# Reordered loads, scatter pacing and joined halves in a four-stage mixture-of-experts kernel

## What is computed

```
x = x + tanh(g0) * E(layernorm(x), token_ids, ctx)      # 4 experts, one per token, weights Wg = Wu = Wd = ctx[e], 512x512
x = x + tanh(g1) * F(layernorm(x))                      # gated FFN, 512 -> 2048 -> 512, Walsh-Hadamard transforms around its weights
x = x + tanh(g2) * R(layernorm(x), ctx)                 # a recurrence along the 512 positions of each sequence, per channel
x = x + tanh(g3) * M(layernorm(x))                      # 8 experts of 512 -> 448 -> 512, top 2 per token, and a shared expert
```

## Time and profile before

| what | value |
|---|---|
| runs | 1247.7, 1248.07, 1249.19 us, median 1248.07 |
| the profiled execution | 1258.69 us, of it the span 1256.9 us |
| PE busy | 1204.7 us, 96% of the span |
| DVE, ACT, POOL busy | 673.6, 453.4, 459.3 us |
| mean DMA rate | 194 GB/s |

### The profile page before, as it was taken

The page is one execution under the profiler, slowest core; times in us unless marked ns, Lnnn a source line. Parts: engine busy times, 40 slices in busy tenths (PEclk is TensorE's granted clock), DMA queues, the critical chain, the costliest instruction groups (busy, mean ns, idle before and its releaser), DMA issues.

```text
span 1256.9 us, 17870 instructions
## 1 busy us (share of the span) xinstructions
PE 1204.7 (96%) x5791; PEld 1012.7 (81%) x5792; DVE 673.6 (54%) x1231; ACT 453.4 (36%) x767; POOL 459.3 (37%) x397
## 2 busy tenths in 40 slices
PE   6799989999999999999999988998899999999998
PEld 6688868888888878888788877887688888888887
DVE  5655479766355665656455646868526333333331
ACT  3433343443234424343244327652122222222222
POOL 2232023000022210321233414353667537986665
PEclk9899999999999999999999999999899999999999
DMA  7842168755659955894786503125454525645553
GB/s 244 305 143 76 43 209 319 275 202 212 256 210 311 339 203 201 293 353 164 253 301 243 181 0 114 47 83 198 190 187 159 168 86 193 209 138 180 179 157 129
DMA packets 64955, 243.61 MB, mean 194 GB/s; under 512 B 8444, under 2 KB 10712, under 8 KB 51192
## 3 DMA queue, kind: packets, MB, share of 16 engines
q1 hardware_dynamic: 41144, 155.93, 33.9%
q0 software_dynamic: 23280, 86.55, 21.2%
q10 hardware_dynamic: 464, 0.27, 0.1%
HBM read 165.13 MB, written 77.59 MB: 193 GB/s over the span
## 4 chain that ended last, share of the span: by engine, by line
PE 82%; DVE 7%; issue 4%; ACT 3%; DMA 3%; POOL 1%; SPq 0%; ACTq 0%; DVEq 0%; POOLq 0%
PE bank L1281 25%; PE bank L1451 18%; PE bank L1307 12%; PE bank L1484 9%; PE bank L1219 4%; PE bank L1240 4%; PE bank L1414 2%; PE bank L1469 2%; PE bank L1262 1%; DMA xres<-in_ctx 1%; DMA wdn<-in_L_ffn_W_down 1%; POOL xs_sorted L824 1%; PE bank L1227 1%; PE bank L1197 1%; PE bank L1316 1%
## 5 line engine op out<-in xcount | busy, mean ns | idle before, releaser
L1281 PE MATMUL bank<-xTh,G 128*128 128x512 f32 x1024 | 272.6, 394 | 0.0
L1281 PEld LDWEIGHTS bank<-xTh,G 128*128 128x128 f32 x1024 | 190.8, 188 | 41.0 <-issue 2.4
L1451 PE MATMUL bank<-W,dxh 128*128 (+2 forms) x880 | 204.6, 373 | 13.5 <-DVE dmid L1942 7.9
L1451 PEld LDWEIGHTS bank<-W,dxh 128*128 128x128 f32 x880 | 161.8, 189 | 29.3 <-issue 15.8
L1307 PE MATMUL bank<-DN,bhh 128*128 128x512 f32 x512 | 158.0, 390 | 0.0
L1281 PE MATMUL bank<-xTl,G 128*128 128x512 f32 x512 | 137.1, 389 | 0.0
L1484 PE MATMUL bank<-W,dhh 128*128 (+1 forms) x440 | 126.9, 411 | 2.3 <-ACT dys L1103 2.1
L1795 DVE SCALAR_TENSOR_TENSOR bs<-bank,tab,bs 128x512 f32<-128x512 f32 x64 | 46.8, 732 | 146.8 <-PE bank L1281 146.8
L1940 DVE TENSOR_TENSOR dmid<-bank,dsg 128x384 f32<-128x384 f32 x55 | 30.5, 555 | 158.3 <-ACT dsg L1093 145.3
L1307 PEld LDWEIGHTS bank<-DN,bhh 128*128 128x128 f32 x512 | 96.1, 188 | 20.8 <-issue 1.0
L1281 PEld LDWEIGHTS bank<-xTl,G 128*128 128x128 f32 x512 | 96.1, 188 | 20.4
(11 more groups left out here) (296 smaller groups left out, 1963.0 us busy)
## 6 DMA issues: line engine op xcount, KB each, us to landing
G<-gate_up_split SPq DMA_DIRECT2D x48, 1024.0 KB, 7.1
DN<-down_split SPq DMA_DIRECT2D x24, 1024.0 KB, 4.9
gate_up_split<-G SPq DMA_DIRECT2D x16, 1024.0 KB, 6.3
wst<-in_L_ffn_w POOLq DMA_DIRECT2D x16, 896.0 KB, 5.6
y_all<-dys SPq DMA_DIRECT2D x55, 256.0 KB, 2.0
xs_sorted<-zero POOLq DMA_DIRECT2D x3, 3328.0 KB, 20.2
xsd<-xs_sorted SPq DMA_DIRECT2D x39, 256.0 KB
down_split<-DN SPq DMA_DIRECT2D x8, 1024.0 KB, 4.3
```

The costliest lines, as they stand in the source:

```text
L1281: mm = pe.matmul(bank[m][:, :], G[:, c % 2, f, h, m, i, :], a[b % 2][:, i, :], start=(n == 0), stop=(n == 3 * DC - 1))
L1451: mm = pe.matmul(bank[o][:, 0:width], a[par][:, k, :], w[:, bass.ds(slot, 1), at + k * step:at + k * step + width].rearrange("p a n -> p ( ...
```

## The change

In stage 1 SP loads all four matrices of ctx before W_down, and only three pieces of W_down before the first tile; PE and ACT run 6 calls of `w16` before the first tile, 6 after the last and 4 after the turns, instead of 10, 4 and 2. DVE runs more of `w_low` before the first tile. POOL computes the first `rstd` before a gather instead of after it, and reads a count earlier. In batches 1 to 3 the input of `mix` is cut into halves on ACT and DVE and multiplied in two `fp32r` matmuls, and the steps of `normal`, `turn` and the second `half_mix` move. In stage 3 the blocks of rows are spread otherwise over the tiles, and `d_hid` of tile 10 moves ahead of `places`. Between stages 3 and 4 the first routed tile waits for part of the scatters only, and PE's order around it changes.

```diff
-        BESIDE = 10
+        BESIDE = 6
...
-            sp.dma_start(nat_at[0], ctx_v[:, 0, :, :]).then_inc(s_ctx[0], 16)
+            for e in range(E0):
+                sp.dma_start(nat_at[e], ctx_v[:, e, :, :]).then_inc(s_ctx[e], 16)
             for n in range(BESIDE // 2):
                 sp.dma_start(wdn_at[n], w_down[:, 8 * n:8 * n + 8, :]).then_inc(s_wdn[n], 16)
-            sp.dma_start(nat_at[1], ctx_v[:, 1, :, :]).then_inc(s_ctx[1], 16)
...
-            sp.wait_ge(s_xg[0], 16)
-            for e in range(2, E0):
-                sp.dma_start(nat_at[e], ctx_v[:, e, :, :]).then_inc(s_ctx[e], 16)
             sp.wait_ge(s_wl, E0 * DC)
-            sp.wait_ge(s_w16, 8)
+            sp.wait_ge(s_w16, BESIDE)
             sp.wait_ge(s_rank, 2)
-            for n in range(BESIDE // 2, 8):
+            for n in range(BESIDE // 2, 7):
...
+                if t == NT0 - 2:                                   # SP, stores of stage 1
+                    sp.wait_ge(s_xn, NT0)
+                    sp.dma_start(wdn_at[7], w_down[:, 56:64, :]).then_inc(s_wdn[1], 16)
...
-            for t in range(TT - 2):                                # SP, stage 3
+            for t in range(TT - 3):
                 store(t)
+            sp.wait_ge(s_slot1, 2)
+            n = sp.value_load(first_i[0:1, 0:1], min_val=1, max_val=4)
+            for i in range(8):
+                sp.wait_ge(s_rsc[i], n * 16)
+            load(TT)
             for i in range(8):
                 sp.wait_ge(s_rsc[i], 16 * 2 * TT // 8)
-            load(TT)
             load(TT + 1)
+            store(TT - 3)
...
-            for j in range(DC):                                    # ACT, stage 1
+            for j in range(E0 * DC):
                 w_high(j)
...
-            for n in range(4):
+            for n in range(BESIDE):
                 w16(n)
-            for n in range(4, 8):
-                w16(n)
-                w_high(n)
             x_high(0)
-            for n in range(8, BESIDE):
-                w16(n)
             x_high(1)
-            for j in range(2 * DC, E0 * DC):
-                w_high(j)
...
+            def mix_high(b, h):                                    # ACT
+                act.wait_ge(s_bq, 2 * b + 2)
+                act.activation(xTh[b % 2][:, 2 * h:2 * h + 2, :], xq[b % 2][:, 2 * h:2 * h + 2, :], ACT.Copy).then_inc(s_xmh, 1)
...
+                if b < NB - 1 and k == (NK - 2 if b == 0 else 11): # ACT, after silu(g)
+                    mix_high(b + 1, 0)
+                    mix_high(b + 1, 1)
...
-            for n in range(2):                                     # PE, before the product of line 1189
-                w16(n)
...
-            for n in range(2, 8):
+            for n in range(BESIDE):
                 w16(n)
             x_turn(0)
-            for n in range(8, BESIDE):
-                w16(n)
             x_turn(1)
...
+                    pe.wait_ge(s_xml, 2 * b - 1 + c // 2)          # PE, mix for b > 0
+                    pe.matmul(bank[bk][:, :], signs[:, :], xTl[b % 2][:, c, :], start=True, stop=False)
+                    pe.matmul(bank[bk][:, :], signs[:, :], xTh[b % 2][:, c, :], start=False, stop=True).then_inc(s_hx, 1)
...
-            for j in range(2, 4):                                  # DVE, stage 1
+            for j in range(2, 7):
                 w_low(j)
             x_stats(0)
-            w_low(4)
+            w_low(7)
             x_norm(0)
             x_stats(1)
             x_low(0)
             x_norm(1)
-            w_low(5)
+            w_low(8)
+            w_low(9)
             x_low(1)
-            for j in range(6, E0 * DC):
+            for j in range(10, E0 * DC):
                 w_low(j)
...
+            def mix_low(b, h):                                     # DVE: xTl half = xq half - xTh half
...
+                if b == 0 and k == NK - 2:                         # DVE, before hidden(g); h = 1 after hidden_low(g)
+                    mix_low(1, 0)
...
+                if 0 < b < NB - 1 and step_at(k, 0) is not None:   # was at step_at(k, 2)
+                    normal(b + 1, step_at(k, 0))
...
-                if b < NB - 1 and k == NK - 3:
+                if b < NB - 1 and k == (NK - 3 if b == 0 else 10):
                     half_mix(b + 1, 1)
                     full_mix(b + 1)
+                if 0 < b < NB - 1 and k == NK - 3:
+                    mix_low(b + 1, 0)
+                    mix_low(b + 1, 1)
...
-                if t > LATE + 1:                                   # DVE, stage 3
-                    rows(4)
+                if t > LATE + 2:
+                    rows(3)
                 d_mul(t)
                 if t == LATE + 1:
+                    d_hid(t - 1)
                     places()
                     rows(4)
+                if t == LATE + 2:
+                    rows(3)
...
-                if t >= 1:
+                if t >= 1 and t != LATE + 1:
                     d_hid(t - 1)
...
-                if t == LATE + 1:
-                    rows(4)
                 if t > LATE + 1:
-                    rows(3)
+                    rows(3 if t % 2 else 4)
+                if t == LATE + 3:
+                    first()                                        # 8 small operations: first_i, for SP
...
             d_down(TT - 1, 1, True)                                # PE, between stages 3 and 4
+            d_up(TT, 0, False)
             d_x(TT + 1, 1)
-            d_up(TT, 0, False)
-            d_x(TT + 2, 0)
+            d_mid(TT, 0)
             pe.wait_ge(s_co, NU)
             d_up(TT + 1, 1, False)
-            d_mid(TT, 0)
+            d_x(TT + 2, 0)
```

More of the change, by code:

```diff
@@ L252, in program @@
         has = place("has", [P, E1, TT], RING + 3072)
+        first_lim, first_cmp, first_n, first_i = run(
+            RING + 3584, ("first_lim", [P, 1]), ("first_cmp", [P, TT]), ("first_n", [P, 1]), ("first_i", [P, 1], I32))
         fetched = [rows_at[2 + i] for i in range(6)]
@@ L320, in program @@
         s_bq = sem("s_bq")
+        s_xmh = sem("s_xmh")
+        s_xml = sem("s_xml")
         s_hx = sem("s_hx")
@@ L391, in program @@
         ctx_v = ctx.rearrange("e (k p) f -> p e k f", p=P)
-        wdn_at = [wdn[:, n, :, :] for n in range(2)] + [wn[m][:, :, :] for m in range(2)] + [wdn_ring[:, :, :]] + [
-            wdn[:, n, :, :] for n in range(2)] + [wdn_lane[:, :, :]]
+        wdn_at = [wdn[:, n, :, :] for n in range(2)] + [wn0[:, :, :]] + [wdn[:, n, :, :] for n in range(2)] + [
+            wdn_lane[:, n, :, :] for n in range(2)] + [wdn_rows[:, :, :]]
         wug_v = [w.rearrange("j p i c n -> j p (i c) n") for w in (w_gate, w_up)]
@@ L1012, in _ @@
             gu_high(0, 1)
-            for n in range(BESIDE, 14):
+            for n in range(BESIDE, 12):
                 w16(n)
@@ L1016, in _ @@
                 turn_high(0, c, 2 + c)
-            for n in range(14, 16):
+            for n in range(12, 16):
                 w16(n)
@@ L1048, in _ @@
                 else:
-                    if b + 1 < NB and step_at(k, 3) is not None:
-                        turn_high(b + 1, step_at(k, 3), 6)
+                    if b + 1 < NB and step_at(k, 1) is not None:
+                        turn_high(b + 1, step_at(k, 1), 6)
                     if b + 1 < NB and k == NK - 1:
@@ L1132, in _ @@
                     act.wait_ge(s_lg, HELD + 1)
-                    act.activation(prob[:, :, :], lg[:, :, :], ACT.Exp).then_inc(s_ex8, 1)
+                    act.activation(prob[:, :, :], lg[:, :, :], ACT.Exp).then_inc(s_lg, 1)
                 if t in VALUE_T[:-1]:
@@ L1141, in _ @@
             d_y(TT - 1)
+            d_gate(TT)
             d_x(TT + 1 + MORE, 1, TT)
-            d_gate(TT)
+            d_hid(TT)
+            d_gate(TT + 1)
             d_x(TT + 2 + MORE, 0, TT + 1)
-            d_gate(TT + 1)
-            d_hid(TT)
             for t in range(TT + 2, TT + NT1):
@@ L1355, in _ @@
                     s = step_at(k, 2)
-                    if b == 1 and s == 0:
-                        pe.wait_ge(s_wdt, 2 * NJ)
-                    elif b + 1 < NB and s > 0:
-                        pe.wait_ge(s_bTh, DC * (b + 1) + s)
-                    elif b + 1 == NB:
+                    if b + 1 < NB:
+                        pe.wait_ge(s_bTh, DC * (b + 1) + s + 1)
+                    else:
                         pe.wait_ge(s_cf, n + s)
                     c_keys(n + s)
-                if b + 1 < NB and b > 0 and step_at(k, 3) is not None:
-                    pe.wait_ge(s_cf, n + step_at(k, 3) + 1)
-                    turn(b + 1, step_at(k, 3), 6)
+                if b + 1 < NB and b > 0 and step_at(k, 1) is not None:
+                    s = step_at(k, 1)
+                    if s > 0:
+                        pe.wait_ge(s_cf, n + s)
+                    else:
+                        pe.wait_ge(s_hxl, DC * (b + 1))
+                    turn(b + 1, s, 6)
                 if b == 0 and k == NK - 1:
@@ L1919, in _ @@
```

(8 more changed lines are left out.)

43 lines of the change are left out of this document (30 added, 13 removed).

## The result

**1238.13 us** (1237.57 to 1239.18, three runs) against 1248.07: ratio 0.9906, 95% interval 0.988 to 0.9933. In a second comparison the unaltered changed kernel had 1239.91 against 1249.42, ratio 0.9932 (0.9911 to 0.9954). The kernel is faster by 9.9 and 9.5 us by the medians, by 11.7 and 8.5 us by the ratios; the forecast was 12.25.

The account below looks back on a forecast made before the run. PE, busy for 96% of the span, was taken to bound the kernel. The terms -3.8 + 1.05 - 4.4 - 5.9 + 0.8 summed to -12.25 us, from 1248.07 to 1235.8 us, with a range of 1231.5 to 1242.

Parts of the forecast that it names:

- term 5: Between stages 3 and 4: 0.45 us wait goes, `d_mid(16)` waits 1.2 us; +0.8 us, between -2 and +1.5.
- Term 1: Start of stage 1: ctx loaded first, turn of tile 2 at 38.4 instead of 42.2; -3.8 us.
- E: Time at which the six `w16` at the start end: 28 us, with bounds 26 and 30.5.
- I leave the half-speed stretch as it was: At the start: PE still idles 4.4 us before tile 2's turn, so the half-speed clock there was assumed unchanged.
- warm start: Rival at the start: idle before tile 2 too short for the clock to fall; sum -15.15, 1232.9 us; chance 0.12.
- cold start: Rival at the start: half speed through all six `w16`, or gathers delay W_down; start gains nothing, 1239.6 us; chance 0.17.
- Term 2: Between stages 1 and 2: six `w16` instead of four after the last tile delay the turns; +1.05 us.
- Term 3: Mixes of batches 1 to 3: twelve float32 mixes become two half matmuls each; -4.4 us, between -5.0 and -3.
- Term 4: Shared tiles 10 to 12 in stage 3: PE's waits for the hidden layer go; -5.9 us, between -6 and -2.
- third rival: Rival on stage 3's waits; includes the first routed tile not being earlier, at less than 1 us; 1241.7 us; chance 0.1.
- the stage-3 waits are not there without the profiler: Rival, tiles 10 to 12: their 5.9 us are not to be had; sum -6.35, 1241.7 us; chance 0.1.
- The ring of rows holds DVE: Rival, tiles 12 to 15: late scatters make each tile wait, 18.7 us instead of 5.97; 1254.4 us; chance 0.05.

Follow-up runs that it names:

- third set: Four runs on one chip: the changed kernel unaltered (1239.91 us), the turns inside, the old rows and the late load; the kernel before took 1249.42 us there.
- first set: Four runs on another chip: the turns inside, the old rows, the late load, and float32 mixes as before (1256.76 us); the kernel before took 1257.78 us there.
- the turns inside: Changed kernel with the turns of tiles 17 and 18 put inside the up products of tiles 16 and 17: 1245.99 us, ratio 0.9905; again 1235.68, 0.9891.
- the old rows: Changed kernel with stage 3's order of rows and hidden-layer step on DVE as before, early first load kept: 1255.55 us, ratio 0.9974; again 1244.59, 0.9957.
- the late load: Changed kernel with the first routed tile's load put back behind all scatters: 1253.16 us, ratio 0.9953; again 1248.23, 0.9985.
- the small cuts: Changed kernel with DVE's small cuts of the last expert weights moved into its idle time at the start: 1238.89 us, ratio 0.9908.

## Why the prediction was right, and where it wasn't

The sign and the range were right; the gain is smaller than forecast by 2.3 us (first comparison). That it is no more is partly luck: term 5 missed by 5.9 us, and the stretches of terms 1, 2 and 4 gave 3.6 us more than forecast, mostly by a clock that fell less than before and that no term had priced. The rivals that were to carry such misses don't name what happened between stages 3 and 4.

**Term 1, the start: right.** The six `w16` end at 28.0 (E = 28), the first of them at half speed as assumed (6.30 us for the 32 matmuls of four calls, 2.02 for the 16 of the last two), and the turn of tile 2 starts at 38.28 (38.4). Before it PE idles for 2.1 us and not 4.4, since tile 0's product started later and ran in part at half clock. What the term left out is the step "I leave the half-speed stretch as it was": the clock between 38 and 48 is 0.83 and not 0.51, which gives 1.1 us more by the turn of tile 3. That is over a third of the 2.9 us of the warm start, and the cold start didn't come. The warm start came in whole elsewhere: of the eleven profiles with this start the clock between 38 and 48 is 0.83 to 0.89 in nine and 1.00 in two, and there stage 1 ends 2.2 us earlier than in the first profile of the changed kernel.

**Term 2, the boundary: wrong in sign by 2 us.** +1.05 forecast, -0.9 measured, by the marks of the table. The turns start 0.8 us later behind stage 1's last product (8.17 us instead of 7.36), near the forecast, and the two more calls do fall into the wait for `xq`, as said. What I didn't price is the clock: with the wait, the mixes behind it ran at half clock in part (5.40 us); without it they take 3.70.

**Term 3, the mixes: right.** -4.4 forecast, -4.1 and -4.2 measured. (Twelve times 0.41 are 4.9 and not 5.0 us.) No wait of PE over 0.4 us in steps 3 to 10; at step 14 of batch 0 it waits 0.4 us for the half, where 0.6 was forecast.

**Term 4, tiles 10 to 12: right in size, with a condition I missed.** 6.4 us go in the stretch of the two waits. The ring of rows holds nearly nobody up: in both profiles of the changed kernel no wait for `dmid` in tiles 12 to 15 is over 0.7 us. DVE does stand at scatters there, for up to 1.9 us at a time, and two kernels with the same stage 3 have a wait of 0.98 and of 1.55 us before the last shared up product; so the slack was as thin as said. But the 6.4 us bring PE to the first routed turn before the scatters are through, which only the early load makes good.

**Term 5, between stages 3 and 4: the step that failed.** +0.8 forecast, +6.7 in the trace. The sum had the wait of `d_mid(16)` (1.2 forecast, 0.99 measured) and stopped there. Behind it `d_x` of tile 18 and the loop's `d_x` of tile 19 stand without a product between them, and DVE's cut of tile 18 stands behind `d_mul(17)`: 1.59 and 0.65 us of wait, then products at half clock. Putting a product between each turn and the next step took back 5.6 us at its place. And the early load, worth 0.45 us in the sum, "-2" as a bound and "less than 1 us" in the third rival, was mis-sized the other way: without it 5.99 us of wait and the clock behind it come back, 6.8 us at its place.

The rival *the stage-3 waits are not there without the profiler* falls by the third set's runs (3.1 to 4.7 us, with no overlap with the changed kernel's lower seven). *The ring of rows holds DVE* falls in its price of 18.7 us; a trace of it is left, as said under term 4.

The sum by the marks: -3.9 - 1.1 - 0.9 - 4.1 - 6.4 + 6.7 = -9.7, measured -9.94 and -9.5. It leaves out a stretch at stage 3's start, from stage 2's last group to the middle step of tile 7: 94.1 us before, 95.3 and 94.9 in the two profiles of the changed kernel, which would make it -8.5. The change doesn't touch it, and the other kernels, all with the same code there, take 94.0 to 96.5 us; what differs is how long PE works at half clock behind two waits that all of them have.

## What to carry to other kernels

When a step of one tile is moved, walk on to the next two tiles on every engine it touches, and look for two steps in a row on the bound engine with no long product between; a wait there costs itself and, mostly, half-clock products behind it. A saving ahead of a point that another queue bounds is worth next to nothing until that queue is earlier too, so price such pairs together and not as a sum. A small piece ("the load may go at 16 scatters, not 32") deserves a look at what happens if it is left out.

## What the hardware showed that I had not expected

**The standstill is not the profiler's alone**, as I had taken it. The first set's chip had it in all four profiles, the chips of the other sets in none of eight; in the first comparison the profile of before had it and that of after had not. Here in the kernel with the early load undone, first set, PE, ACT and DVE, 10.75 us without work on PE and then 3.32 us for eight matmuls that take 1.9:

```profile
883.75 0.54 ACT L1098 ACTIVATE dsg<-bank 128x448 f32<-128x448 f32 x1 [16.43 <-remote]
...
884.33 0.56 DVE L1965 TENSOR_TENSOR dmid<-bank,dsg 128x384 f32<-128x384 f32 x1 [10.58 <-ACT dsg L1098]
...
885.23 3.32 PE L1462 MATMUL bank<-W,dxh 128*128 128x448 f32 x8 [10.75 <-DVE dmid L1967]
```

By the brackets PE waits for DVE, DVE for ACT, and ACT for a releaser that the profile calls `remote` and names no further. All five profiles with a standstill have such a wait of ACT, of 10.7 to 16.4 us, and none of the nine others has one, which points at ACT as the first that stands. For the first six us POOL still issues a scatter every 1.27 us, then it waits for a block of rows from DVE. Runs timed without a profile were longer on that chip too, which fits a standstill in them but doesn't show it: 10.3 us for the turns inside (1245.99 and 1235.68), 11.0 for the old rows, 8 to 9 for the kernel before, but 4.9 for the late load, whose 6 us of wait the standstill hides in its profile. What holds ACT, and why on some chips, is open.

**An addition on DVE stretches while POOL multiplies, and a row load of stage 4 comes late behind it.** Four of the twelve profiles have a wait of 1.8 to 2.0 us for a row load with half-clock products behind, about 4 us in all, three of them near 1075 to 1087 and one at 998; in the rest no row load of stage 4 keeps PE waiting over 0.8 us. The traces show what makes the load late. Here the kernel with the small cuts, DVE, POOL and SP's queue ahead of its wait at 1075.48:

```profile
1064.30 5.14 DVE L2173 TENSOR_TENSOR xres<-row,xres 128x512 f32<-128x512 f32 x1
1064.80 4.08 POOL L710 TENSOR_TENSOR W<-wst,W 128x1792 fp32r<-128x1792 f32 x1
1069.47 0.32 SPq L559 DMA_DIRECT2D row<-y_all  x1
1069.83 0.43 SPq L530 DMA_DIRECT2D xsd<-xs_sorted  x1
```

The addition `xres<-row,xres` takes 0.69 us at its shortest. In these four places it takes 4.68 to 5.33 us and ends about half a microsecond behind POOL's `W<-wst,W`; at 1013.89 of the same profile, where POOL's began 1.2 us earlier, it takes 3.42 us and again ends half a microsecond behind it. Elsewhere in these profiles it takes 0.69 to 2.0 us. SP issues `row<-y_all` only when the addition is done, and the row load stands behind that in SP's queue, 3.3 us late. In the second profile of the changed kernel the same addition (1068.23) takes 0.69 us and is over before POOL's begins at 1069.27. So a shift of a microsecond between DVE and POOL decides over 4 us, which is enough to hide an edit of 4 us in six runs. No run takes the addition or POOL's product away from there, so this is read from the traces and not tried.

**Half clock follows waits shorter than I thought.** A wait of 3.15 us ahead of the mixes, or of 1.6 and 0.65 us in a row between two turns, is followed by matmuls at half clock (5.40 us instead of 3.70; 3.15 instead of 1.89). With what follows, each cost one and a half times its length or more (3.15 + 1.70; 2.24 + 1.6). It is not so every time: behind the same 1.58 us between the two turns, the first set's kernel with the old rows takes 1.88 us for the eight matmuls; and behind the wait of 3.2 us at stage 3's start, which all profiles have, eight matmuls take anything from 1.88 to 3.14 us. So the half-clock share of a price may be absent in the next run.
